# Rows of x fetched already turned, and normalised with features on the partitions, in a layernorm + FFN + Golay kernel

## The reference

```python
x = L0_attn_x                                   # (2, 4096, 256) float32: 8192 rows of 256
xn = (x - mean(x)) / sqrt(var(x) + 1e-5)        # over the 256 features
# attention part
D = clip(log-log slope over prefixes of 4..1024 values of xn, 1, 2)   # one number
x1 = real(ifft(fft(xn) * filt(D)))              # a 256x256 circulant matrix, made from D
bits = (sigmoid(x1 @ W_el + b_el) > 0.5)        # 24 bits per row
corrected = golay_correct(bits)                 # flips up to 3 bits by the syndrome
attn = x1 + corrected @ W_le + b_le
# FFN part
ffn = gelu(xn @ w1 + b1) @ w2 + b2              # 256 -> 1024 -> 256
out = x + attn + ffn
```

## Time and profile before

| | |
|---|---|
| time, median of 3 runs | 452.41 us (452.39 to 452.6) |
| profiled execution, first to last instruction | 451.6 us (the page gives no other time of it) |
| busy TensorE, weight loads | 98%, 89% |
| busy VectorE, ScalarE, GpSimd | 58%, 44%, 6% |
| DMA | 19.58 MB, 43 GB/s over the span |

### The profile page before, as it was taken

One profiled execution on the slowest core, in us unless ns is written; L12 is line 12 of the kernel. 1 busy time (PEld: TensorE's weight loads), 2 busy tenths in 40 slices (PEclk: granted clock), 3 DMA queues, 4 the chain that ended last, 5 costly groups with the idle time before them and its releaser, 6 DMA issues.

```text
span 451.6 us, 8842 instructions
## 1 busy us (share of the span) xinstructions
PE 444.3 (98%) x2976; PEld 402.1 (89%) x2976; DVE 260.4 (58%) x752; ACT 196.5 (44%) x332; POOL 26.5 (6%) x42
## 2 busy tenths in 40 slices
PE   6999999999999999999999999999999999999996
PEld 3889998988999899998998999899898999989896
DVE  5888556465554646547465564746547465564544
ACT  4744444344443543444444343544345434443431
POOL 1601001010000101001010010100001010010000
PEclk9999999999999999999999999999999999999999
DMA  7788100000000000000000000000000000000101
GB/s 227 210 263 248 59 25 25 0 23 23 23 23 23 0 23 23 23 23 23 0 23 23 23 23 14 10 23 23 23 23 15 8 23 23 23 23 0 48 25 47
DMA packets 11308, 19.58 MB, mean 43 GB/s; under 512 B 2691, under 2 KB 4893, under 8 KB 11293
## 3 DMA queue, kind: packets, MB, share of 16 engines
q1 hardware_dynamic: 11298, 19.44, 13.0%
HBM read 11.03 MB, written 8.39 MB: 43 GB/s over the span
## 4 chain that ended last, share of the span: by engine, by line
PE 97%; DMA 1%; DVE 0%; ACT 0%; SPq 0%; issue 0%; DVEq 0%
PE p_o L739 41%; PE p_h L719 39%; PE p_c L753 11%; PE p_t L690 3%; PE p_c L772 2%; DMA w_f<-L_ffn_w 1%; PE p_g L763 1%; PE p_c L827 0%; DVE x_sb L544 0%; PE p_c L837 0%; SPq L214 0%; ACT w_hi L360 0%; DVE x_sb L502 0%; ACT xT_hi L374 0%; SPq L224 0%
## 5 line engine op out<-in xcount | busy, mean ns | idle before, releaser
L319 ACT ACTIVATE h<-p_h,b_sb 128x512 f32<-128x512 f32 x128 | 88.1, 688 | 226.3 <-PE p_h L719 226.2
L450 DVE TENSOR_TENSOR h_lo<-h,h_hi 128x512 fp32r<-128x512 f32 x128 | 90.0, 704 | 110.6 <-ACT h_hi L327 108.7
L739 PE MATMUL p_o<-w_hi,h_hi 128*128 128x256 f32 x512 | 149.7, 292 | 0.0
L739 PE MATMUL p_o<-w_lo,h_hi 128*128 128x256 f32 x512 | 144.5, 282 | 0.0
L739 PE MATMUL p_o<-w_hi,h_lo 128*128 128x256 f32 x512 | 144.4, 282 | 0.0
L739 PEld LDWEIGHTS p_o<-w_hi,h_hi 128*128 128x128 f32 x512 | 97.3, 190 | 2.2 <-DVE h_lo L450 0.5
L739 PEld LDWEIGHTS p_o<-w_lo,h_hi 128*128 128x128 f32 x512 | 97.5, 191 | 1.3
L739 PEld LDWEIGHTS p_o<-w_hi,h_lo 128*128 128x128 f32 x512 | 97.4, 190 | 0.0
L719 PE MATMUL p_h<-xT_hi,w_hi 128*128 128x512 f32 (+1 forms) x258 | 82.1, 399 | 0.8 <-ACT xT_hi L374 0.8
L327 ACT CAST h_hi<-h 128x512 fp32r<-128x512 f32 x128 | 79.6, 622 | 5.6
L719 PE MATMUL p_h<-xT_hi,w_lo 128*128 128x512 f32 (+1 forms) x258 | 79.8, 390 | 0.0
(11 more groups left out here) (95 smaller groups left out, 314.2 us busy)
## 6 DMA issues: line engine op xcount, KB each, us to landing
out<-x_sb SPq DMA_DIRECT2D x31, 256.0 KB, 2.0
x_sb<-L_attn_x SPq DMA_DIRECT2D x15, 512.0 KB, 4.0
w_f<-L_ffn_w SPq DMA_DIRECT2D x3, 512.0 KB, 8.2
x_sb<-L_attn_x SPq DMA_DIRECT2D x2, 256.0 KB, 3.1
w_f<-L_ffn_w SPq DMA_DIRECT2D x2, 256.0 KB, 5.8
basis_sb<-basis SPq DMA_DIRECT2D x1, 256.0 KB, 5.0
out<-x_sb SPq DMA_DIRECT2D x2, 128.0 KB, 1.8
con<-consts SPq DMA_DIRECT2D x1, 144.5 KB, 3.4
```

The lines of the kernel that those rows point to most:

```text
L319: nc.scalar.activation(h[m % 2][:], p_h[:, m % 2, :], ACT.Gelu, bias=b1_sb[:, m:m + 1]).then_inc(gelu_done, 1)
L450: nc.vector.tensor_tensor(h_lo[m % HR][:], h[m % 2][:], h_hi[m % HR][:].bitcast(F32), ALU.subtract).then_inc(h_lo_done, 1)
L739: last = mm(p_o[:, j, :], hp[r][:, tok], w[:, m, :], start=(m == 0 and n == 0 and j % 2 == 0), stop=(m == MB - 1 and n == 2), skip_group_c ...
```

## The change

The host passes a second copy of x, `xt`, with the features of each chunk on the partitions (a layout change without arithmetic). SP loads chunk c of it, 512 KB, into one of two buffers `xt_sb`. The inverse root is written into the variance's place in `mv`. SP then stores `mv` of the chunk (128 partitions x 8 values, 4 KB) to DRAM, waits for it, and loads these 1024 values into each of the 128 partitions of `rows_sb` (512 KB). VectorE subtracts the means (`centre`, two instructions of 128x512) and multiplies by the roots (`scale`, two more), in place in `xt_sb`. Their second operand steps through `rows_sb` by 8 values (32 bytes) from token to token. ScalarE and VectorE make `xT_hi` and `xT_lo` from `xt_sb` instead of from PSUM. `transpose_block` and `p_t` are gone; chunk 0 is still transposed by TensorE (L851). SP's loads are no longer all early: the order is unrolled over the chunks.

```diff
+        xt_sb = [sb(f"xt_sb{i}", [P, KB, CTOK], F32) for i in range(2)]
+        rows_sb = [sb(f"rows_sb{i}", [P, P, CT, 2], F32) for i in range(2)]
-        p_t = ps("p_t", [P, BANK], F32)
+        rows_dram = nc.dram_tensor("rows_dram", (2, P, CT * 2), F32, kind="Internal").ap()
+        def nth(c, par):
+            return 8 * (c + par)
@@ SP
+            def load_xt(c):
+                if c > 2:
+                    sp.wait_ge(t_lo, KB * (c - 1))
+                sp.dma_start(xt_sb[c % 2][:, :, :], xt[c * P:(c + 1) * P, :]).then_inc(xt_in[c % 2], 16)
+            def load_x(c):
+                par = c % 2
+                sp.wait_ge(x_in[par], 8 * (c - par))
+                cols = slice(c * CW, (c + 1) * CW)
+                sp.dma_start(x_sb[:, cols], x_rows[:, cols]).then_inc(x_in[par], 16)
+            def spread_rows(c):
+                par = c % 2
+                sp.wait_ge(rstd_done, c + HEAD + 1)
+                if c > 2:
+                    sp.wait_ge(rows_in[par], nth(c - 2, par))
+                sp.dma_start(rows_dram[par], mv[par][:, :, :].rearrange("p j a -> p (j a)")).then_inc(rows_out[par], 16)
+                sp.wait_ge(rows_out[par], nth(c, par))
+                if c > 2:
+                    sp.wait_ge(scaled, KB * (c - 2))
+                sp.dma_start(rows_sb[par][:, :, :, :].rearrange("p t j a -> p (t j a)"),
+                             rows_dram[par].rearrange("t a -> (t a)").partition_broadcast(P)).then_inc(rows_in[par], 16)
+            load_xt(1)           # after the five fr_x loads
+            spread_rows(1)       # after basis, wel and mask; then bel, le_f
-            with sp.Fori(1, CHUNKS // 2) as i:
...
-            with sp.Fori(0, (CHUNKS - 1) * PAIRS) as n:
...
+            load_x(2)
+            load_xt(2)
+            load_x(3)
+            for c in range(1, CHUNKS - 1):
+                if c + 2 < CHUNKS:
+                    load_xt(c + 2)
+                spread_rows(c + 1)
+                if c + 3 < CHUNKS:
+                    load_x(c + 3)
+                for q in range(PAIRS):
+                    store_pair(c - 1, q)
+            for q in range(PAIRS):
+                store_pair(CHUNKS - 2, q)
@@ GpSimd, inverse_root
-                nc.gpsimd.tensor_tensor(rstd[par][:, tiles], var_eps[:, tiles], minus_half[:, tiles],
+                nc.gpsimd.tensor_tensor(mv[par][:, tiles, 1], var_eps[:, tiles], minus_half[:, tiles],
@@ ScalarE, transposed_hi
-                act.wait_ge(t_done, KB * c + k + 1)
-                nc.scalar.copy(xT_hi[par][:, k, :], p_t[:]).then_inc(t_hi, 1)
+                act.wait_ge(scaled, KB * (c - 1) + k + 1)
+                if not isinstance(c, int) or c > 1:
+                    act.wait_ge(wave_done, PAIRS * (c - 1))
+                nc.scalar.copy(xT_hi[par][:, k, :], xt_sb[par][:, k, :]).then_inc(t_hi, 1)
@@ VectorE
+            def row_values(par, a):
+                return rows_sb[par][:, :, :, a].rearrange("p t j -> p j t")
+            def centre(c, par):
+                dve.wait_ge(xt_in[par], nth(c, par))
+                dve.wait_ge(rows_in[par], nth(c, par))
+                for k in range(KB):
+                    seg = xt_sb[par][:, k, :].rearrange("p (j t) -> p j t", j=CT)
+                    nc.vector.tensor_tensor(seg, seg, row_values(par, 0), ALU.subtract).then_inc(centred, 1)
+            def scale(c, par):
+                for k in range(KB):
+                    dve.wait_ge(centred, KB * (c - 1) + k + 1)
+                    seg = xt_sb[par][:, k, :].rearrange("p (j t) -> p j t", j=CT)
+                    nc.vector.tensor_tensor(seg, seg, row_values(par, 1), ALU.mult).then_inc(scaled, 1)
@@ VectorE, chunk
                 hidden_lo(c, 3)
-                normalise(c + 1, 1 - par)
+                centre(c + 1, 1 - par)
                 add_wave(c - 1, 0)
                 hidden_lo(c, 4)
+                scale(c + 1, 1 - par)
                 hidden_lo(c, 5)
@@ VectorE, chunk 0
-            normalise(1, 1)
+            centre(1, 1)
             hidden_lo(0, 5)
+            scale(1, 1)
@@ TensorE, chunk, and twice in chunk 0
-                    if m >= 6:
-                        transpose_block(c + 1, m - 6)
@@ host
+    rows = np.asarray(inputs["L0_attn_x"]).reshape(P, CHUNKS, CT, KB, P)
+    turned = rows.transpose(1, 4, 3, 2, 0).reshape(CHUNKS * P, KB * CTOK)
```

More of the change, by code:

```diff
@@ L76, with build @@
 K_END = K_POW2 + LAT
-def build(nc, x, w_el, b_el, w_le, b_le, w1, b1, w2, b2, consts, prefixes, basis, masks, out):
+def build(nc, x, xt, w_el, b_el, w_le, b_le, w1, b1, w2, b2, consts, prefixes, basis, masks, out):
     ctx = ExitStack()
@@ L117, in build @@
         var_eps = sb("var_eps", [P, CT], F32)
-        rstd = [sb(f"rstd{i}", [P, CT], F32) for i in range(2)]
         eps = sb("eps", [P, CT], F32)
@@ L159, in build @@
         x_head = sem("x_head")
+        xt_in = [sem("xt_even"), sem("xt_odd")]
+        rows_out = [sem("rows_out_even"), sem("rows_out_odd")]
+        rows_in = [sem("rows_in_even"), sem("rows_in_odd")]
+        centred, scaled = sem("centred"), sem("scaled")
         w1_in = [sem(f"w1_in{i}") for i in range(len(W1_PARTS))]
@@ L230, in _, with store_pair @@
             load_w1(2)
+            def load_xt(c):
[18 more added lines that the diff above has]
+                             rows_dram[par].rearrange("t a -> (t a)").partition_broadcast(P)).then_inc(rows_in[par], 16)
+            def store_pair(c, q):
+                sp.wait_ge(pair_out, PRIMED + PAIRS * c + q + 1)
+                cols = slice(c * CW + q * 2 * E, c * CW + (q + 1) * 2 * E)
+                sp.dma_start(out_rows[:, cols], x_sb[:, cols]).then_inc(stored, 16)
             sp.dma_start(x_sb[:, CW:2 * CW], x_rows[:, CW:2 * CW]).then_inc(x_in[1], 16)
@@ L244, in _ @@
             sp.dma_start(le_f[LAT + 1:LAT + 2, :], b2[None, :]).then_inc(le_in, 16)
-            with sp.Fori(1, CHUNKS // 2) as i:
[L246 to L250, removed]
-            with sp.Fori(0, (CHUNKS - 1) * PAIRS) as n:
-                sp.wait_ge(pair_out, PRIMED + n + 1)
-                sp.dma_start(out_rows[:, bass.ds(n * (2 * E), 2 * E)],
-                             x_sb[:, bass.ds(n * (2 * E), 2 * E)]).then_inc(stored, 16)
+            load_x(2)
[11 more added lines that the diff above has]
+                store_pair(CHUNKS - 2, q)
             for n, (j0, j1) in enumerate(LAST_PIECES):
@@ L425, in aggregate, with normalise_first @@
                 last.then_inc(stat_done, 1)
[L427 to L439, removed]
-                last.then_inc(xn_done, 1)
+            def normalise_first(g):
+                dve.wait_ge(rstd_done, g + 1)
+                for j in range(g * HALF, (g + 1) * HALF):
+                    last = nc.vector.tensor_scalar(xn[:, j, :], x_chunk(0)[:, j, :], mv[0][:, j, 0:1],
+                                                   mv[0][:, j, 1:2], ALU.subtract, ALU.mult)
+                last.then_inc(xn_done, 1)
+            def row_values(par, a):
[11 more added lines that the diff above has]
+                    nc.vector.tensor_tensor(seg, seg, row_values(par, 1), ALU.mult).then_inc(scaled, 1)
             def transposed_lo(c, par, k):
                 dve.wait_ge(t_hi, KB * c + k + 1)
-                nc.vector.tensor_tensor(xT_lo[par][:, k, :], p_t[:], xT_hi[par][:, k, :].bitcast(F32),
+                nc.vector.tensor_tensor(xT_lo[par][:, k, :], xt_sb[par][:, k, :], xT_hi[par][:, k, :].bitcast(F32),
                                         ALU.subtract).then_inc(t_lo, 1)
@@ L565, in _ @@
                 aggregate(0, halves[g])
-            normalise(0, 0, 0)
-            normalise(0, 0, 1)
+            normalise_first(0)
+            normalise_first(1)
             w1_part_lo(0)
@@ L681, in _ @@
             mm = nc.tensor.matmul
[L683 to L692, removed]
             def up(c, par, m, first=False):
@@ L861, in _ @@
                     down(0, m - 2, first=True)
-                if m == 6:
-                    transpose_block(1, 0)
             down(0, MB - 2)
-            transpose_block(1, 1)
             circulant()
@@ L916, in constants @@
     return con, prefixes, basis, masks
-_INS = ["L0_attn_x", "L0_attn_W_el", "L0_attn_b_el", "L0_attn_W_le", "L0_attn_b_le",
+_INS = ["L0_attn_x", "xt", "L0_attn_W_el", "L0_attn_b_el", "L0_attn_W_le", "L0_attn_b_le",
         "L0_ffn_w1", "L0_ffn_b1", "L0_ffn_w2", "L0_ffn_b2"]
@@ L929 @@
     arrays, args = {}, []
+    rows = np.asarray(inputs["L0_attn_x"]).reshape(P, CHUNKS, CT, KB, P)
+    turned = rows.transpose(1, 4, 3, 2, 0).reshape(CHUNKS * P, KB * CTOK)
     for name in _INS:
-        arrays[name] = np.ascontiguousarray(inputs[name])
+        arrays[name] = np.ascontiguousarray(turned if name == "xt" else inputs[name])
     for name, a in zip(("consts", "prefixes", "basis", "masks"), constants()):
```

## The result

The changed kernel takes 470.75 us (median of 4 runs, 468.72 to 474.3), the kernel before 452.5 us (4 runs, 452.39 to 453.12). The ratio is 1.0408, with a 95% interval of 1.0365 to 1.0451. The forecast was 463.4 us in a range of 442 to 478: the side is right, the slowdown of 11 us was sized too small, it is 18 us.

A forecast was written before the change was run, and what follows sets the result against it. TensorE was taken as the bound. Each of 14 periods changes by -0.88 + 1.43 = +0.55 us, together +7.7; chunk 0 adds 3.3; span 451.6 becomes 462.6, plus 0.8 gives 463.4 us, range 442 to 478.

The forecast's parts named there:

- TensorE bounds the kernel, 0.44 us a block comes off: TensorE, whole run: 30 transpose blocks of 0.44 us go, 13.2 us in all, 0.88 in each period.
- The add behind centre becomes the wait that ends last: Chunk bodies: add_wave, queued behind centre on VectorE, makes TensorE's second wave_products wait 1.43 us in each period.
- The root is made 7.4 us into the period, the store leaves at once: Chunk bodies: root made by 152.57 in the period from 145.14; SP issues the store 0.08 us later.
- The store of 4 KB, 1.7 us: SP storing mv to DRAM: lands after 1.7 us, with ends of 1.5 and 2.8.
- The spread load, 3.2 us: SP loading the 4 KB into all partitions of rows_sb: takes 3.2 us, with ends of 3.0 and 4.7.
- One strided instruction, 1.15 us from start to start: Each centre or scale instruction on VectorE: 1.15 us, chosen at 2 to 1 over the dense rate's 0.61.
- The rest of the period is hidden: Chunk bodies: scale, the hidden_lo work, correct, ScalarE's copies and the xt loads add nothing to the period.
- Chunk 0, 3.3 us: Chunk 0: centre and scale hold VectorE 4.6 us instead of 1.30, so TensorE reaches the circulant 3.3 us later.
- The rival: Chunk 0: TensorE's clock falls to 1.2 GHz after a pause, adding 2 to 4 us, 466; no separate chance given.
- The span to the time, 0.8 us: Whole kernel: the median of the runs lies 0.8 us above the profiled span, added to reach the forecast time.

The follow-up runs named there:

- e3: Changed kernel with add_wave(c-1, 0) put ahead of centre(c+1) on VectorE in the 14 chunk bodies; 444.13 us, ratio 0.9815.
- e2: Changed kernel with load_x(c+3) issued after the chunk's first store instead of 0.4 us behind the spread load; 460.02 us, ratio 1.0157.
- e9: Changed kernel with the second operand stepping by 8 bytes in centre and 16 in scale instead of 32 (wrong values); 454.77 us, one run.
- e7: Changed kernel with rows_sb loaded before the root is waited for, from a constant table (wrong values), store kept; 444.02 us, ratio 0.9807.
- e4: Changed kernel with 14 bf16 matmuls of zeros ahead of down(0, 6) in chunk 0, where TensorE paused; 469.49 us, ratio 1.0356.
- e6: Changed kernel with 14 zero matmuls in chunk 0 and 8 more ahead of the second wave_products in each body; 469.32 us, ratio 1.0371.
- e1: Changed kernel with centre and scale reading 512 side-by-side values of rows_sb instead of 32 bytes apart (wrong values); 453.35 us, ratio 1.0017.

## Why the prediction was right, and where its sum was short

- *TensorE bounds the kernel, 0.44 us a block comes off.* Right: e3's period is 27.27 - 0.86.
- *The add behind centre becomes the wait that ends last.* Right, and shown by e3: moving the add alone gives the whole wait back.
- *The root is made 7.4 us into the period, the store leaves at once.* Right: 159.53 - 152.07 = 7.46 against 7.51.
- *The store of 4 KB, 1.7 us.* 1.43 us, 0.3 less. My lower end of 1.5 was too high: 32-byte pieces were nothing to fear.
- *The spread load, 3.2 us.* **This is the term that was mis-sized: 4.15 us.** I had argued that nothing is ahead of it and counted load_x behind it as nothing. e2 shows that it is load_x: issued later, the load takes 3.4. The rows landed 13.1 us into the period, not 12.5. Where the two misses meet, the weight load is 1.9 us late instead of 1.43; a period costs 0.85 and not 0.55, 14 x 0.30 = 4.2 us. The 0.46 us at the weight load became 0.30 by a second, smaller error of the other sign: the sum took the weight load's lateness for TensorE's loss, but before, that load ran 0.39 us ahead of its matmuls (159.27 and 159.66), and now they start together. Counted at the matmuls, this period loses 16.02 - 14.52 = 1.50 us, the twelve take 1.82 instead of 1.55, and 0.88 comes off: 0.89.
- *One strided instruction, 1.15 us from start to start.* Right: 1.15 to 1.18 long, 1.1 from start to start. It was a choice between two rows, and the reason that I gave for it was wrong, so that it came out was luck: e9's step of 8 bytes walks the same 4096 bytes and takes 0.69 us. What counts is the step.
- *The rest of the period is hidden.* Right: in e3 and e7 TensorE has no idle time in a period.
- *Chunk 0, 3.3 us.* Chunk 1 starts at 39.12 instead of 35.78, 3.3 us later, but by two parts. The circulant slipped 2.4 us (34.94 against 32.58), as VectorE came to centre at 24.4 and not at 25.0 and the pairs took 4.3 and not 4.6; the clock's fall added 0.9 (the circulant took 2.07 us instead of 1.13). The rival had the fall and put it at 2 to 4 us. So the 3.3 of the sum is met by luck: its slip was 0.9 too long, and the fall was not in it.
- *The clock in the bodies.* Not in the sum, and no rival spoke of it: the one on the clock looked at chunk 0 alone. The profiled run had only the fall in chunk 0. Over the runs the clock is 0.996, 0.992, 0.989, 0.986, for spans of 466.8, 468.6, 469.1 and 472.4 us, and no trace shows where the clock fell in the last three. e4's trace shows a fall behind a wait in a body, e6 with the waits filled has none in four runs, and e1, whose matmuls wait 0.9 us at most in a body, none in ten. That ties such falls to the waits, with few runs. But e7's run at 0.992 has one long fall in chunk 0 and no wait in a body, so a part of what the low clocks stand for may be there. The middle of the runs is 2.0 us above the profiled span.
- *The span to the time, 0.8 us.* It is 1.9 us in the four runs of the changed kernel and 1.7 to 2.0 in all others, before too (a run of the kernel before with a span of 450.6 takes 452.5). I had set the span of one run against the median of others; with 1.9 us the profiled run of before would have taken 453.5, 1.0 more than the median. That is an error of 1.1 us.

The sum by these: 466.8 - 451.6 = 15.2 us between the two profiles (3.3 in chunk 0 and 14 x 0.85), 2.0 from the profiled run to the middle one, put down to its falls, and 1.0 as the profiled run of before was longer than the median: 18.2, of 18.25 measured. The first is read from traces; the second is a difference of whole runs, and its cause is only argued.

## What to carry to other kernels

When work is taken off the bounding engine and handed to another, look at what is queued behind the new wait on that engine, and put first whatever the bounding engine is waiting for: one swap of two calls here is worth 26.6 us and turns a ratio of 1.041 into one of 0.981. A transfer on such a path should have no other transfer issued behind it either, and an operand should be laid out so that its step stays under 16 bytes. A wait on TensorE that comes back in every stage can cost more than its length, as its clock may fall behind it: waits of some 1.5 us a period did so in some runs here, those of up to 0.9 us (e1) in none of ten.

## What the runs showed of the hardware

- VectorE, tensor_tensor of 128x512 float32 in SBUF, second operand with a step of 4 or 8 bytes: 0.69 us; 16 bytes: 1.09; 32 bytes: 1.16 to 1.18.
- A store of 128 pieces of 32 bytes to DRAM lands 1.43 us after its issue, faster than the 128 KB store's 1.7. The load of one 4 KB piece into all 128 partitions lands in 3.4 us (median of e2) without another load behind it and in 4.2 with a 512 KB load issued 0.4 us behind it.
- TensorE's granted clock fell to 0.50 for 3.4 us after pauses of 2.9 us (chunk 0), 2.5 us (e3, chunk 0) and 1.8 us (e4, one wait of fourteen), and for 6.8 us after one of 3.3 us (e7, chunk 0). Runs of e4 with a fall took 1.7 to 2.0 us more than the one without, but in e7 two runs at 0.996 took only 0.2 to 1.0 more than two without one. bf16 matmuls of zeros in the pauses keep the clock at 0.999 and above.
